# Split 256-column products for the key block that two query tiles share, in a windowed-attention block on one core

## What is computed

```python
x = x + attn(layernorm(x))            # rotary q and k, then
#   valid = (k_pos > q_pos - 128) & (k_pos <= q_pos)
#   attn  = softmax(where(valid, q @ k.T / sqrt(128), min));  out = attn @ v;  out @ wo
x = x + ffn(layernorm(x))             # ternary w1, exact gelu, ternary w2
```

## Time and profile before

| | us |
|---|---|
| median of 3 runs | 361.02 (360.62 to 361.49) |
| the profiled execution | 360.54 |
| its span in the profile | 358.8 |
| busy: PE | 340.5 |
| busy: DVE | 263.8 |
| busy: POOL | 223.5 |
| busy: ACT | 208.1 |

### The profile page before, as it was taken

How to read it: one execution, slowest core, us unless ns; L and a number is a source line. 1 busy time by engine, 2 the same in 40 slices (tenths; PEclk the granted TensorE clock), 3 DMA queues, 4 the chain that set the end, 5 groups by cost and what they waited for, 6 DMA issues and landing times.

```text
span 358.8 us, 6923 instructions
## 1 busy us (share of the span) xinstructions
PE 340.5 (95%) x2410; PEld 315.1 (88%) x2410; DVE 263.8 (74%) x607; ACT 208.1 (58%) x626; POOL 223.5 (62%) x182
## 2 busy tenths in 40 slices
PE   7849999999999999999999999999999999898996
PEld 6738778999999999999999999999999999877986
DVE  4874777668766886788788986787678766788681
ACT  2243676677777556655665566556665666365180
POOL 2326778667767678799879987585867656231300
PEclk9997999999999999999999999999999999999999
DMA  7734466543333333333333333333322231000001
GB/s 220 188 95 114 117 164 197 130 102 78 92 83 86 80 84 84 88 81 89 88 90 88 90 88 90 90 89 90 88 61 58 61 88 31 0 3 0 31 29 58
DMA packets 29025, 31.25 MB, mean 87 GB/s; under 512 B 3392, under 2 KB 20288, under 8 KB 28992
## 3 DMA queue, kind: packets, MB, share of 16 engines
q1 hardware_dynamic: 28992, 30.82, 33.7%
HBM read 12.98 MB, written 1.05 MB: 39 GB/s over the span
## 4 chain that ended last, share of the span: by engine, by line
PE 84%; DVE 9%; POOL 2%; issue 2%; DMA 1%; ACT 1%; DVEq 0%; SPq 0%; POOLq 0%
PE PR L385 22%; PE OT L460 15%; PE VO L400 13%; PE SC L435 12%; PE VO L417 11%; PE PT L446 3%; PE PR L488 2%; PE SC L488 2%; PE VO L507 1%; DVE probsT L765 1%; PE SC L507 1%; DVE stats L690 1%; DVE SC L751 1%; DVE gT_lo L807 1%; DVE gT_lo L772 1%
## 5 line engine op out<-in xcount | busy, mean ns | idle before, releaser
L954 POOL TENSOR_TENSOR gT_lo<-turn,gT_hi 128x512 fp32r<-128x512 f32 x62 | 81.7, 1318 | 42.9 <-ACT gT_hi L589 42.7
L949 POOL TENSOR_TENSOR turn<-turn,swapped 128x512 f32<-128x512 f32 x62 | 80.2, 1293 | 38.2 <-DMA swapped<-by_sin 37.9
L594 ACT ACTIVATE probs<-SC,negmax 128x128 f32<-128x128 f32 x128 | 45.8, 363 | 61.9 <-DVE negmax L754 61.9
L460 PE MATMUL OT<-probsT,v_sb 128*128 128x128 f32 x480 | 64.6, 276 | 3.1 <-DVE gT_lo L772 2.7
L601 ACT ACTIVATE probs<-probs,rinv 128x128 f32<-128x128 f32 x128 | 44.5, 395 | 38.2 <-DVE rinv L759 38.2
L460 PEld LDWEIGHTS OT<-probsT,v_sb 128*128 128x128 f32 x480 | 58.9, 191 | 6.0 <-DVE probsT L765 6.0
L385 PE MATMUL PR<-xT_hi,qk_lo 128*128 128x512 f32 x128 | 56.2, 439 | 5.1 <-POOL qk_lo L936 3.7
L751 DVE COPY_PREDICATED SC<-in_prev_sb,SC 128x256 f32<-128x256 int32 x48 | 20.6, 428 | 45.7 <-PE SC L435 45.5
L385 PE MATMUL PR<-xT_hi,qk_hi 128*128 128x512 f32 x128 | 51.0, 398 | 0.0
L385 PE MATMUL PR<-xT_lo,qk_hi 128*128 128x512 f32 x128 | 50.4, 394 | 0.0
L765 DVE TENSOR_TENSOR probsT<-PT,mask_sb 128x512 f32<-128x512 f32 x64 | 43.6, 681 | 1.2 <-PE PT L446 1.2
(11 more groups left out here) (114 smaller groups left out, 839.1 us busy)
## 6 DMA issues: line engine op xcount, KB each, us to landing
swapped<-by_sin SPq DMA_DIRECT2D x128, 128.0 KB, 2.3
qk_raw<-in_wq SPq DMA_DIRECT2D x16, 128.0 KB, 2.6
qk_raw<-in_wk SPq DMA_DIRECT2D x16, 128.0 KB, 2.4
v_raw<-in_wv SPq DMA_DIRECT2D x8, 256.0 KB, 3.1
o_raw<-in_wo SPq DMA_DIRECT2D x8, 256.0 KB, 2.9
xres<-in_x SPq DMA_DIRECT2D x4, 256.0 KB, 3.2
w_raw<-in_w1t SPq DMA_DIRECT2D x4, 256.0 KB, 3.0
w_raw<-in_w2t SPq DMA_DIRECT2D x4, 256.0 KB, 3.0
```

The costliest lines, as they stand in the source:

```text
L460: last = mm(OT[:, i * P:(i + 1) * P], v_sb[:, t - 1 + b, a * HD:(a + 1) * HD], probsT[:, i, b], start=(b == b0), stop=(b == 1))
L594: nc.scalar.activation(probs[n % 2][:, i], SC[n % 2][:, i * 256 + P:(i + 1) * 256], ACT.Exp, bias=negmax[:, n % 2, i:i + 1], accum_out=row ...
L949: tt(turn[m % 4][:], turn[m % 4][:], swapped[m % 2][:], ALU.add).then_inc(rot_done, 1)
L954: tt(rot_lo(head, c % 2)[:, half_of(c)], turn[m % 4][:], rot_hi(head, c % 2)[:, half_of(c)].bitcast(F32), ALU.subtract).then_inc(rotlo_don ...
```

## The change

A step's two query tiles 2j and 2j+1 share the key tile 2j: it is the first one's own block and the second one's earlier block. Both parts of the probabilities lie side by side in `probsT` (256 columns). The changed kernel weighs this shared tile for both queries at once with three split products of 256 columns; the other two key tiles (odd ones) stay plain float32 products of 128 columns. For that

- value tiles with even numbers are kept as `v_even_hi` and `v_even_lo`, those with odd numbers as `v_odd` in float32: `copy_v` on ScalarE becomes two copies of 256 columns, and `v_low` on VectorE takes the lower half from the bank (32 times); the bank is free only after that,
- `pt_hi` on ScalarE copies the shared 256 columns of `probsT` to `both_hi`, after the step's exponentials,
- `pt_lo` on GpSimd takes the lower half into `both_lo`, after the step's `rotate`,
- `weigh_v` waits for `both_hi` ahead of its first product and for `both_lo` ahead of its last.

```diff
             def weigh_v(n):
                 head, j = step(n)
                 a = head % 2
-                pe.wait_ge(pt_masked, n + 1)
-                pe.wait_ge(v_copied, 4 * (head // 2) + j + 1)
+                hs = slice(a * HD, (a + 1) * HD)
+                pe.wait_ge(v_split, 4 * (head // 2) + j + 1)
                 if n > 0:
                     pe.wait_ge(otlo_done, n)
-                for i in range(2):
-                    t = 2 * j + i
-                    b0 = 1 if t == 0 else 0
-                    for b in range(b0, 2):
-                        last = mm(OT[:, i * P:(i + 1) * P], v_sb[:, t - 1 + b, a * HD:(a + 1) * HD],
-                                  probsT[:, i, b], start=(b == b0), stop=(b == 1))
+                pe.wait_ge(both_hi_done, n + 1)
+                mm(OT[:, 0:256], v_even_hi[:, j, hs], both_hi[:], start=True, stop=False)
+                mm(OT[:, 0:256], v_even_lo[:, j, hs], both_hi[:], start=False, stop=False)
+                if j > 0:
+                    mm(OT[:, 0:P], v_odd[:, j - 1, hs], probsT[:, 0, 0], start=False, stop=False)
+                mm(OT[:, P:256], v_odd[:, j, hs], probsT[:, 1, 1], start=False, stop=False)
+                pe.wait_ge(both_lo_done, n + 1)
+                last = mm(OT[:, 0:256], v_even_hi[:, j, hs], both_lo[:], start=False, stop=True)
                 last.then_inc(pv_done, 1)
...
             def copy_v(v):
                 c = v % 4
                 act.wait_ge(v_done, v + 1)
-                copy(v_sb[:, 2 * c:2 * c + 2], VO[v % 2][:].rearrange("p (t n) -> p t n", t=2)).then_inc(v_copied, 1)
+                copy(v_even_hi[:, c], VO[v % 2][:, 0:256])
+                copy(v_odd[:, c], VO[v % 2][:, 256:512]).then_inc(v_copied, 1)
+
+            def pt_hi(n):
+                act.wait_ge(pt_masked, n + 1)
+                copy(both_hi[:], probsT[:].rearrange("p i b q -> p (i b q)")[:, P:3 * P]).then_inc(both_hi_done, 1)
...
                 exps(n)
                 if n == STEPS - 1:
                     xt_hi(1, 0)
+                    pt_hi(n - 1)
                     ot_hi(n - 1)
                     nc.scalar.preload_act_table(ACT.Gelu)
                 if n > 0:
+                    if n < STEPS - 1:
+                        pt_hi(n - 1)
                     for kind, i in fills(n - 1):
...
             for k in range(2 * NF):
                 gelu(k)
                 if k == 1:
+                    pt_hi(STEPS - 1)
                     ot_hi(STEPS - 1)
...
+            def v_low(v):
+                c = v % 4
+                dve.wait_ge(v_copied, v + 1)
+                tt(v_even_lo[:, c], VO[v % 2][:, 0:256], v_even_hi[:, c].bitcast(F32), ALU.subtract).then_inc(v_split, 1)
...
             rotlo(0)
+            v_low(0)
+            v_low(1)
             rotate(1)
...
                 if 0 < n < LP + 4:
                     for kind, w in fills(n - 1):
-                        if kind == "o":
-                            add_out(w)
+                        (add_out if kind == "o" else v_low)(w)
...
+            def pt_lo(n):
+                pool.wait_ge(both_hi_done, n + 1)
+                tt(both_lo[:], probsT[:].rearrange("p i b q -> p (i b q)")[:, P:3 * P], both_hi[:].bitcast(F32),
+                   ALU.subtract).then_inc(both_lo_done, 1)
...
                 rotlo(n + 2)
                 if n + 3 < CHUNKS:
                     rotate(n + 3)
+                if n > 0:
+                    pt_lo(n - 1)
                 if s == 2 and p < PAIRS - 1:
                     qklo(2 * p + 2)
...
+            pt_lo(STEPS - 3)
             rsqrt(1, 0)
+            pt_lo(STEPS - 2)
+            pt_lo(STEPS - 1)
```

More of the change, by code:

```diff
@@ L73, in preln_block_kernel @@
         probsT = sb("probsT", [P, 2, 2, P])
-        v_sb = sb("v_sb", [P, NT, 2 * HD])
+        both_hi = sb("both_hi", [P, 2 * P], F32R)
+        both_lo = sb("both_lo", [P, 2 * P], F32R)
+        v_odd = sb("v_odd", [P, NT // 2, 2 * HD])
+        v_even_hi = sb("v_even_hi", [P, NT // 2, 2 * HD], F32R)
+        v_even_lo = sb("v_even_lo", [P, NT // 2, 2 * HD], F32R)
         gT_hi = sb("gT_hi", [P, NF, T], F32R)
@@ L164, in preln_block_kernel @@
         v_copied = sem("v_copied")
+        v_split = sem("v_split")
+        both_hi_done = sem("both_hi_done")
+        both_lo_done = sem("both_lo_done")
         wo_done = sem("wo_done")
@@ L370, in bank_free @@
                 if user is not None:
-                    pe.wait_ge(*((v_copied, user[1] + 1) if user[0] == "v" else (wo_added, o_at[user[1]] + 1)))
+                    pe.wait_ge(*((v_split, user[1] + 1) if user[0] == "v" else (wo_added, o_at[user[1]] + 1)))
             def project(m, split=None):
```

## The result

The changed kernel takes 378.45 us (median; 372.88 to 381.87) against 360.82 (359.92 to 361.49) for the kernel before in the same comparison: ratio 1.037, interval 1.030 to 1.043. It is slower, as forecast, but the median lies 9.4 us above the forecast and 4.9 above the upper end of the range; the mean of those two, 374.0, lies 5.0 and 0.5 above. The profiled execution took 375.15 (span 373.1); before, 360.54 (span 358.8).

The account below looks back on a forecast made before the run. TensorE, 95% busy, bounds the kernel, but GpSimd's late subtraction would stall it: -3.6 saved, +0.75, +2.5, +4.0, +2.5 and +2.1 added to 360.54 give 368.8, set to 369.0 us; range 363.0 to 373.5.

Parts of the forecast that it names:

- the late rotations: Filled steps outside steps 25 to 40: late DMA swaps delay rotation and subtraction, TensorE stalls; +4.0 us, ends 0.2 and 6.1.
- steps 25 to 41: Forecast as steps 25 to 40: GpSimd, also thresholding weight pieces, becomes the pace; +2.5 us, between -1.4 and +4.3.
- the end: Last steps: tile 62's copy stands behind two 512-column copies, delaying the last weighing and all behind; +2.1 us, ends 1.2 and 2.5.
- the saving: Shorter weighing on TensorE saves 0.09 us a step, kept by 40 steps: -3.6 us.
- The likeliest case: GpSimd's queue paces the weighing, because the last product waits for the subtraction behind the rotation; 369.0 us, chance 0.70.
- The products: Weighing on TensorE: three split products and two f32 products take 0.80 us instead of 0.89.
- Rival D: Weighing products don't get shorter, since switching between split and f32 costs another 0.08 us; 372.5 us, chance 0.12.
- Rivals B and C: B: subtraction covered in every filled step, 358.9, chance 0.12; C: same cover, full prices without fill and at end, 361.4, 0.06.
- Start and steps 2 to 6: VectorE's two queued subtractions delay the start, +0.75 us; steps without fill wait for copy and subtraction, +2.5 us.
- The test for one step: TensorE stalls if rotation end + 0.69 + 0.1 exceeds weighing start + 0.68 (0.46 in a head's first step).
- two hits in three fetches: A swap is in flight 2.8 of 4.6 us, so about two in three instruction fetches make one late; 4.0 us taken.
- The sentence on the Trainium skill: VectorE and GpSimd operations reading SBUF block each other, so all eight pairs of steps 25 to 40 are caught: nearer +4.

Follow-up runs that it names:

- the reordered start: Changed kernel with the subtraction on VectorE, the two value subtractions behind the first rotations and tile 62's copy ahead of the two 512-column copies: 368.78 us, ratio 1.024.
- the shifted stream: Changed kernel with 24 unused products of 8 columns (96 instructions) added to TensorE's stream in step 0: 374.24 us, a single run.
- the ternary elsewhere: Changed kernel with VectorE's eight ternary operations moved from even steps 26 to 40 to odd steps 43 to 57: 371.45 us, ratio 1.029.
- the second trace: Profile of the changed kernel run once more, unaltered, beside the other kernels: median 378.24 us, ratio 1.044 to the kernel before.
- that order and the waits covered: Changed kernel with weighing behind next scores, thresholds every fourth step, start and end reordered, ternary one step later in odd steps: 358.52 us, ratio 0.994.

## Why the prediction was right and wrong

Of the 9.4 us between forecast and median, 3.1 are the late rotations, 1.4 the steps 25 to 41, 1.2 the end, 0.4 the saving, which four steps fewer keep, and 3.3 that the median lies above the profiled execution.

**The bound and the mechanism held.** The likeliest case, that GpSimd's queue paces the weighing, is what the traces show. With the subtraction left out the loss is gone, and with the subtraction made but not waited for by TensorE the long steps are gone.

**The products** held: 0.80 from the first weighing product to the scores when nothing is late (143.11 to 143.91 in the last rows), and 0.09 saved in each clean step. Rival D, products that don't get shorter, falls. Rivals B and C, a covered subtraction, fall with the 11.5 us of waits.

**Start and steps 2 to 6** held, +0.9 and +2.4 against +0.75 and +2.5. The start's term is shown by the reordered start, which takes it away.

**The late rotations** are the largest miss of the sum: 7.1 measured against 4.0 taken, above the 6.1 that stood as upper end. The test for one step was right: for step 24 it gives 142.89 + 1.27 + 0.79 = 144.95 against 142.83 + 0.68 (first weighing product at 142.83), a stall of 1.4; the step is 1.5 longer than its usual 4.53. That fetches make the swaps late was right too, as the shifted stream shows. The step that failed is the count of hits: "two hits in three fetches" was taken off the 6.1 that seven hits had cost (two thirds give 4.0), but these seven were already what had struck. Eleven fetches fall into steps 7 to 24 and 42 to 59 of the changed kernel, counting one at the end of step 6; two in three make seven hits, and at 6.1/7 = 0.87 each 6.4 us (estimate). Measured were nine hits and 7.1. The upper end, the hits as they had been, left no room for more. And the term has no fixed size: a shift of 96 instructions takes it from 7.1 to 2.4, as it depends on when a fetch falls after a swap's issue. So the upper end had to allow for every fetch.

**Steps 25 to 41.** The pair of steps at 9.65 was worked out to the hundredth (9.2 and one stretched operation of 0.45); measured 4.76 + 4.89 = 9.65. The number of pairs was mis-sized: five of eight were taken, and nearly all of them pay. With the ternary elsewhere the same GpSimd work costs 78.11 instead of 81.67: of the 5.5 us above the kernel without the subtraction (76.18), 3.6 come from the two engines holding each other up and 1.9 from the count of operations. The sentence on the Trainium skill ("SBUF — State Buffer", section "Who interferes with whom"), nearer +4 when GpSimd is fuller, was the better estimate of this term.

**The end** was right in its chain: +3.3 for steps 60 to 62 and the end, against 2.1 with 2.5 as upper end. The idle time ahead of the weighing of tile 62 was foreseen, the lower clock behind it was not. It added 0.7: in the second trace, where the clock stays up there, the end costs +2.6.

**Not foreseen: the longer runs.** The sum set the median 0.5 above the profiled execution, as before the change; it lies 3.3 above. In the second trace of the changed kernel (379.36 us) one ternary lasts 4.45 us and steps 27 and 28 take 7.04 and 6.08; in the first the longest is 1.95. The two runs near 381.8 have no trace, so what made them long is not shown. The prediction had a longest ternary of 1.66 and no row that showed one held over several operations. Moving the ternary off GpSimd's full steps takes the long ternaries away in the traces, and the runs lie closer together; how often they strike in runs without a trace is not shown.

**What stays open.** Why the packet in step 24 strikes at 2.7 us after the swap's issue (in the second trace of the changed kernel at 2.8, with the same effect), where others at 2.4 to 3.2 don't; and why the clock falls behind the idle time at the end in some executions only.

## What to carry to other kernels

Before a small operation on a side engine is put between two of the busiest engine's steps, look at the latest time that this engine's queue ever stood there, not at its share of busy time: a lateness that nobody waited for becomes a stall in full. Where a VectorE operation with both inputs in SBUF and a GpSimd queue without gaps meet, move the one to where the other rests before judging anything else; here the changed kernel loses 18 us, and with that order and the waits covered it gains 2. A cost that hangs on where background fetches fall is bounded by the number of fetches, not by the hits that one trace shows.

## What the runs showed of the hardware

- A ternary on VectorE with two inputs in SBUF, 0.74 us alone, lasted 4.53 and 5.05 us beside three and four GpSimd operations in a row, and ended some 0.5 us after the last of them. The Trainium skill, "SBUF — State Buffer", section "Who interferes with whom", says that the second of two such operations blocks until the first finishes; held for one operation of 1.3 us it would last some 2 us at most (estimate: 1.3 + 0.74). The changed kernel's median, 1.73, agrees; the longest rows show that it can be held for several.
- Behind an idle time of TensorE of 2.2 us at the end the granted clock was 0.50 for 3.4 us, with eight 512-column products at 0.43 us each instead of 0.23, in the first trace of the changed kernel. In its second trace the same idle time was followed by the full clock. The difference is 0.7 us.
- 96 more instructions on TensorE, put where it was idle, made its instruction fetches of 16 KB come 0.5 to 3 steps earlier in the program and moved the long steps of 7 to 24 and 42 to 59. A fetch that starts 0.5 to 2.0 us after a swap's issue made the swap take 3.5 to 4.6 us instead of 2.8; one that starts 2.4 us or more after it did not, but for one case.
